# Attention scores on 64-row tiles: a pair of heads in two banks instead of against half-empty keys

## The chip, the core and the metric

The kernel runs on one core of a Trainium2 chip. Times are microseconds of device time. The core has five engines that run side by side and meet through semaphores: TensorE (PE in the rows; its weight loads are PEld), VectorE (DVE), ScalarE (ACT), GpSimd (POOL) and SyncE (SP), which issues DMAs. TensorE writes to PSUM, which has eight banks of 512 floats per partition.

## What is computed

Eight sequences of 256 tokens with 128 channels go through one causal attention layer (16 heads of 8 channels) and then through six layers of local attention and a gated feed-forward. The change lies in the local attention:

```python
# per layer: 16 heads, DIM_HEAD 64, WINDOW 32, n = 256 tokens, QK_SCALE 8
q = l2norm(q) * qs ; k = l2norm(k) * ksc          # then rotary tables on both
bk2, bv2 = look(bk), look(bv)                     # each window sees the one before and itself: 64 keys
mask = (it < jb) | (it > jb + w) | (jb == -1)
sim = jnp.einsum('bhwie,bhwje->bhwij', bq, bk2) * QK_SCALE
sim = jnp.where(mask, -jnp.finfo(sim.dtype).max, sim)
attn = jax.nn.softmax(sim, -1)
out = jnp.einsum('bhwij,bhwje->bhwie', attn, bv2)
```

## The kernel before

A first stage (to about 260 us) computes the causal attention and prepares the weights of the six layers: split in two parts for the projections, the value weights folded with the output weights. Then come 48 units, one for each layer and sequence, `u = (m, s)`. Every engine has a hand-written `step(m, s)` that lists its work for several units at once: while unit `u` makes its scores, `after` is already projected, `before` is in its softmax and values, and `last` is in the feed-forward. The steps of all 48 units are written out one behind the other, and nothing but this order and the semaphores decides when something runs.

In a unit tokens are handled in two tiles `t` of 128. For each: `proj` (L1462 to L1464) makes queries, keys and values in 512-column pieces in the two projection banks; ScalarE squares them (`sq`, L1283), VectorE multiplies by the rotary tables (`rot`, L1136) and sums squares (`ssum`, L1112), GpSimd turns and normalises (L1031, L1050 to L1056, L1072), and `transpose_qk` (L1479) turns each pair of heads over into the bank TP. A pair is 128 rows: 64 channels of one head above 64 of the other. ScalarE copies these out: queries to `qT` (L1305), keys to `kT` (L1311).

The keys are stored twice as wide as they are. `kT` is `[P, 2, PAIRS, WIN + T]`: plane 0 holds the first head's keys in rows 0 to 63 and zeros below, plane 1 the second head's in rows 64 to 127 and zeros above. So one matmul over all 128 rows and 128 columns of keys gives both heads' scores side by side:

```python
out_s = ps[32 * k:32 * k + 32, SO[t] + a // 4, (a % 4) * P:(a % 4 + 1) * P]
last = M.matmul(out_s, qT[:, par, a, 32 * w:32 * w + 32], kT[:, :, a, 32 * w:32 * w + 64], ...)
```

`scores(u, t)` does that for 8 pairs `a` and 4 windows `k`; each window's 32 queries are one 32-column strip of the array. Every float32 matmul is two instructions in the trace (x64 for the 32 of a call). Ahead of them two matmuls in bf16 (L1492), one on rows 0 to 63 and one on rows 64 to 127, write the mask into the two banks `SO[t]` and `SO[t] + 1`, and the scores are added to it. A call waits for the copy of the keys (`qkT_a`) and for the output of the unit before to have left the bank (`o_a`, L1338).

The softmax runs in PSUM and `prob`: VectorE takes the maxima (L1147), subtracts them (L1156), ScalarE takes the exponentials back into the banks (L1319), VectorE sums (L1164, L1166) and scales into `prob` (`soft_scale`, L1173). `transpose_p` (L1507) turns `prob` over pair by pair and `values` (L1518) multiplies with the values. The feed-forward has three products with the first weights (`feed_w1`, L1568), each followed by `gate` on ScalarE (L1377) and `hid` on VectorE (L1214), and `feed_w2` (L1579). The fold of the first stage (L726) multiplies 64-row halves of two weights, the two halves in turn, into two banks.

## Time and profile before

| | us |
|---|---|
| median of 3 runs | 1781.34 (1781.17 to 1782.97) |
| the profiled execution | 1780.26 |
| its span, first to last instruction | 1778.4 |
| TensorE busy | 1708.9 (96%) |
| VectorE busy | 1512.6 (85%) |
| GpSimd busy | 1355.7 (76%) |
| ScalarE busy | 1350.4 (76%) |
| DMA, mean | 149 GB/s |

Busy time is the share in which at least one instruction of the engine is recorded. The ends of matmuls are modelled, so the distance from one start to the next tells more of TensorE than its busy share; the chain of work that ended last gives each instruction the time to the next step, so its rows can be added up. In the rows below, the first number of a timeline or chain row is the start, the second the duration.

### The profile page before, as it was taken

What the parts mean: (1) busy time and instruction counts of PE and PEld (TensorE: products, weight loads), DVE (VectorE), ACT (ScalarE), POOL (GpSimd) and SP (SyncE); (2) the same over time, 40 slices, a digit from 0 to 9 for tenths busy, and PEclk for the clock granted to TensorE, in tenths of its full rate; (3) what the DMA queues carried; (4) which work ended last, traced back from release to release, by engine and by line L of the source; (5) the groups of instructions that cost most, each with busy time, mean ns of one, the idle gap of its engine ahead of it and who ended that gap; (6) DMA issues with size and microseconds to landing.
All of it is one profiled execution on the core that took longest, in us unless ns stands there. A gap on an engine that the chain in (4) does not pass through costs nothing.

```text
span 1778.4 us, 53112 instructions
## 1 busy us (share of the span) xinstructions
PE 1708.9 (96%) x20416; PEld 1355.0 (76%) x20416; DVE 1512.6 (85%) x2297; ACT 1350.4 (76%) x2689; POOL 1355.7 (76%) x2035
## 2 busy tenths in 40 slices
PE   7999968999999999999999999999999999999986
PEld 5666646888888888788888788887888888888864
DVE  5666648999999999999999999999899999999973
ACT  6777846787777777787777788787777887777763
POOL 6767658878788787778878787878878787887850
PEclk9999989999999999999999999999999999999996
DMA  3567706465865646765566656558464666656462
GB/s 115 184 234 262 254 10 159 107 148 120 223 141 132 145 107 139 213 143 139 123 147 191 152 123 146 124 127 236 112 161 104 149 177 168 147 117 146 109 152 63
DMA packets 101340, 264.54 MB, mean 149 GB/s; under 512 B 26720, under 2 KB 34912, under 8 KB 101088
## 3 DMA queue, kind: packets, MB, share of 16 engines
q1 hardware_dynamic: 101088, 261.13, 57.8%
q8 instruction: 164, 2.69, 0.7%
q14 instruction: 88, 0.72, 0.1%
HBM read 45.02 MB, written 27.26 MB: 41 GB/s over the span
## 4 chain that ended last, share of the span: by engine, by line
PE 81%; issue 2%; DVE 1%; ACT 1%; POOL 1%; POOLq 0%; ACTq 0%; DVEq 0%
PE ps L1462 12%; PE ps L1497 10%; PE ps L1479 10%; PE ps L1464 10%; PE ps L1463 10%; PE ps L1518 9%; PE ps L1568 7%; PE ps L1507 5%; PE ps L1579 3%; PE ps L1492 2%; PE ps L1537 1%; PE ps L1545 1%; DVE rot L1136 1%; PE ps L1554 1%; PE ps L1529 1%
## 5 line engine op out<-in xcount | busy, mean ns | idle before, releaser
L1136 DVE TENSOR_TENSOR rot<-ps,rope_l 128x1024 f32<-128x1024 f32 x384 | 461.8, 1213 | 100.9 <-ACT sq L1283 84.8
L1031 POOL TENSOR_TENSOR rot<-rot 128x512 f32<-128x512 f32 x384 | 485.8, 1288 | 31.5 <-DVE rot L1136 31.5
L1293 ACT ACTIVATE un<-ps 128x512 f32<-128x512 f32 x384 | 224.6, 598 | 237.9 <-PE ps L1464 229.8
L1462 PE MATMUL ps<-w_t,xs_hi 128*128 128x512 f32 x768 | 374.9, 488 | 12.5 <-DVE rot L1136 7.6
L1072 POOL TENSOR_TENSOR rot<-rot,rnorm 128x1024 f32<-128x1024 f32 x192 | 365.5, 1904 | 21.3
L1464 PE MATMUL ps<-w_t,xs_lo 128*128 128x512 f32 x768 | 304.7, 397 | 0.0
L1463 PE MATMUL ps<-w_t,xs_hi 128*128 128x512 f32 x768 | 303.6, 395 | 0.0
L1283 ACT ACTIVATE sq<-ps 128x512 f32<-128x512 f32 x384 | 229.1, 597 | 34.6 <-PE ps L1464 20.1
L1311 ACT ACTIVATE kT<-ps 64x512 f32<-64x512 f32 x384 | 226.3, 589 | 23.7 <-PE ps L1479 20.3
L1479 PE MATMUL ps<-ident_s,rot 128*128 128x128 f32 x1536 | 234.8, 275 | 8.6 <-ACT kT L1311 3.4
L1112 DVE TENSOR_REDUCE ssum<-sq 128x16 f32<-128x1024 f32 x192 | 232.5, 1211 | 9.8 <-ACT sq L1283 9.8
L1479 PEld LDWEIGHTS ps<-ident_s,rot 128*128 128x128 f32 x1536 | 182.1, 140 | 65.4 <-issue 28.6
L1462 PEld LDWEIGHTS ps<-w_t,xs_hi 128*128 128x128 f32 x768 | 145.7, 190 | 67.9 <-issue 28.8
L1518 PE MATMUL ps<-vk,pT 128*32 128x128 f32 x6144 | 188.3, 275 | 0.0
L1497 PE MATMUL ps<-kT,qT 128*32 128x128 f32 x6144 | 187.6, 274 | 0.0
L1050 POOL TENSOR_TENSOR newton<-rnorm 128x32 f32<-128x32 f32 x288 | 68.6, 238 | 147.3 <-DVE rnorm L1122 132.3
L1497 PEld LDWEIGHTS ps<-kT,qT 128*32 128x32 f32 x6144 | 161.8, 110 | 21.7 <-issue 21.7
L1518 PEld LDWEIGHTS ps<-vk,pT 128*32 128x32 f32 x6144 | 162.3, 110 | 16.7 <-issue 16.3
L1464 PEld LDWEIGHTS ps<-w_t,xs_lo 128*128 128x128 f32 x768 | 145.1, 189 | 33.8
L1568 PE MATMUL ps<-xg,w_s 128*128 128x256 f32 (+1 forms) x576 | 151.9, 387 | 4.5 <-DVE hid L1214 3.5
L1463 PEld LDWEIGHTS ps<-w_t,xs_hi 128*128 128x128 f32 x768 | 147.2, 192 | 8.0
L1568 PEld LDWEIGHTS ps<-xg,w_s 128*128 128x128 f32 (+1 forms) x576 | 103.3, 180 | 32.6 <-DVE hid L1214 5.9
(121 smaller groups left out, 3093.2 us busy)
## 6 DMA issues: line engine op xcount, KB each, us to landing
vk<-un SPq DMA_DIRECT2D x1440, 128.0 KB, 2.3
w_t<-weights_dram SPq DMA_DIRECT2D x48, 512.0 KB, 6.9
weights_dram<-u_split SPq DMA_DIRECT2D x12, 1024.0 KB, 5.1
weights_dram<-qk_split SPq DMA_DIRECT2D x24, 512.0 KB, 4.0
raw<-wqk_dram SPq DMA_DIRECT2D x24, 256.0 KB, 4.9
wvt_s<-wvt_dram SPq DMA_DIRECT2D x12, 256.0 KB, 4.3
wo_s<-wo_dram SPq DMA_DIRECT2D x12, 256.0 KB, 4.7
w_s<-w_dram SPq DMA_DIRECT2D x6, 341.0 KB, 3.8
```

The costliest lines, as they stand in the source:

```text
L1031: last = G.tensor_tensor(cos[:, :, s, :], cos[:, :, s, :], sin[:, :, 1 - s, :], ALU.add)
L1072: G.tensor_tensor(v, v, rnorm[:, t, kind * H:(kind + 1) * H, None].broadcast_to([P, H, D]), ALU.mult).then_inc(nrm_g.sem, 1)
L1112: V.tensor_reduce(ssum[:, t, kind * H:(kind + 1) * H], sq[:, kind, :].rearrange("p (h e) -> p h e", h=H), AX_X, ALU.add).then_inc(ss_d.sem, 1)
L1136: V.tensor_tensor(dst, src[:, None, :, :].broadcast_to([P, 2, H // 2, D]), tab[:, :, None, :].broadcast_to([P, 2, H // 2, D]), ALU.mult).t ...
L1283: S.activation(sq[:, kind, half * 512:(half + 1) * 512], ps[:, PJ + PJ_BANK[t][2 * kind + half], :], ACT.Square).then_inc(sq_a.sem, 1)
L1462: M.matmul(bank, x_hi, w_t[:, j, 0, :], start=True, stop=False)
L1463: M.matmul(bank, x_hi, w_t[:, j, 1, :], start=False, stop=False)
L1464: last = M.matmul(bank, x_lo, w_t[:, j, 0, :], start=False, stop=True)
L1479: last = M.transpose(ps[:, TP, a * P:(a + 1) * P], rot[:, kind, 0, c * P:(c + 1) * P], ident_s[:, :])
L1497: last = M.matmul(out_s, qT[:, par, a, 32 * w:32 * w + 32], kT[:, :, a, 32 * w:32 * w + 64], start=False, stop=a % 4 == 3)
L1518: last = M.matmul(ps[32 * k:32 * k + 32, SO[t], 0:C], pT[:, a, 32 * k:32 * k + 32], vk[:, 4 * t + k, a, :], start=a == 0, stop=a == PAIRS - 1)
L1568: last = M.matmul(ps[0:rows, FB, g * T:(g + 1) * T], w1_s[:, g * DI + at:g * DI + at + rows], xg[:, :], start=True, stop=True)
```

## The change

The keys lose their empty halves: `kT` is `[P, PAIRS, WIN + T]`, and both heads' keys are copied in one instruction. The mask and the scores are computed per window and per head half, each instruction on 64 rows and 32 columns of the array. A head half has a bank of its own (`SO[t] + hp`), so the banks' order is now head half, pair, key, where it was pair, head half, key. `soft_scale` puts `prob` back into the old order, so that what follows finds it as before. The maxima, sums and reciprocals stay in the banks' order on both sides. Only the part that is zeroed in front of the first window of the keys remains of the two memsets.

```diff
-        kT = sb("kT", [P, 2, PAIRS, WIN + T])
+        kT = sb("kT", [P, PAIRS, WIN + T])
...
-                    G.memset(kT[:, 0, :, :], 0.0)
-                    G.memset(kT[:, 1, :, :], 0.0)
+                    G.memset(kT[:, :, 0:WIN], 0.0)
...
-                    V.tensor_tensor(prob[:, t, :].rearrange("p (h k) -> p h k", h=H), tile_scores(t),
-                                    linv[:, t, :, None].broadcast_to([P, H, 2 * WIN]), ALU.mult).then_inc(pn_d.sem, 1)
+                    pairs = prob[:, t, :].rearrange("p (a hp k) -> p hp a k", hp=2, a=PAIRS)
+                    inv = linv[:, t, :].rearrange("p (hp a) -> p hp a", hp=2)[:, :, :, None].broadcast_to([P, 2, PAIRS, 2 * WIN])
+                    V.tensor_tensor(pairs, tile_scores(t).rearrange("p (hp a) k -> p hp a k", hp=2), inv, ALU.mult).then_inc(pn_d.sem, 1)
...
-                        for hp in range(2):
-                            rows = slice(64 * hp, 64 * hp + 64)
-                            last = S.activation(kT[rows, hp, pairs, WIN + t * P:WIN + (t + 1) * P], src[rows], ACT.Copy)
+                        last = S.activation(kT[:, pairs, WIN + t * P:WIN + (t + 1) * P], src, ACT.Copy)
...
-                    for hp in range(2):
-                        rows = slice(64 * hp, 64 * hp + 64)
-                        M.matmul(ps[:, SO[t] + hp, :], wpick[rows, t, :], wmask[rows, :, :].rearrange("p a k -> p (a k)"), start=True, stop=False)
+                    for k in range(4):
+                        for hp in range(2):
+                            rows = slice(64 * hp, 64 * hp + 64)
+                            M.matmul(ps[32 * k:32 * k + 32, SO[t] + hp, :], wpick[rows, t, 32 * k:32 * k + 32], wmask[rows, :, :].rearrange("p a k -> p (a k)"),
+                                     start=True, stop=False)
                     for a in range(PAIRS):
                         for k in range(4):
                             w = 4 * t + k
-                            out_s = ps[32 * k:32 * k + 32, SO[t] + a // 4, (a % 4) * P:(a % 4 + 1) * P]
-                            last = M.matmul(out_s, qT[:, par, a, 32 * w:32 * w + 32], kT[:, :, a, 32 * w:32 * w + 64],
-                                            start=False, stop=a % 4 == 3)
+                            for hp in range(2):
+                                rows = slice(64 * hp, 64 * hp + 64)
+                                out_s = ps[32 * k:32 * k + 32, SO[t] + hp, a * 2 * WIN:(a + 1) * 2 * WIN]
+                                last = M.matmul(out_s, qT[rows, par, a, 32 * w:32 * w + 32], kT[rows, a, 32 * w:32 * w + 64],
+                                                start=False, stop=a == PAIRS - 1)
```

On TensorE, around the first call of `scores` in a unit: the first hidden-layer product, the masks, the scores and the two projections behind them. Before:

```order
L1568 MATMUL ps<-xg,w_s 128x256 [waits xh_d,w1_in]
L1568 MATMUL ps<-xg,w_s 128x256
L1492 MATMUL ps<-wmask,wpick 128x512 [waits o_a,qkT_a]
L1492 MATMUL ps<-wmask,wpick 128x512
L1497 MATMUL ps<-kT,qT 32x128 x32
L1462 MATMUL ps<-w_t,xs_hi 128x512 [waits rope_d]
L1463 MATMUL ps<-w_t,xs_hi 128x512
L1464 MATMUL ps<-w_t,xs_lo 128x512
```

After, at the same place (the lines below L1310 have moved by two, L1492 is L1491, L1497 is L1499, L1568 is L1570):

```order
L1570 MATMUL ps<-xg,w_s 128x256 [waits xh_d,w1_in]
L1570 MATMUL ps<-xg,w_s 128x256
L1491 MATMUL ps<-wmask,wpick 32x512 [waits o_a,qkT_a]
L1491 MATMUL ps<-wmask,wpick 32x512 x7
L1499 MATMUL ps<-kT,qT 32x64 x64
L1460 MATMUL ps<-w_t,xs_hi 128x512 [waits rope_d]
L1461 MATMUL ps<-w_t,xs_hi 128x512
L1462 MATMUL ps<-w_t,xs_lo 128x512
```

Nothing moved; two masks became eight and 32 matmuls of 128 columns became 64 of 64.

On ScalarE, between the exponentials of the first token tile and the copy of the values: the last bank of keys, which the second call of `scores` waits for, and the output `o`. Before:

```order
L1319 ACTIVATE ps<-prob 128x1024 [waits sub_d]
L1311 ACTIVATE kT<-ps 64x4x128 [waits sc_p,qkT_p]
L1311 ACTIVATE kT<-ps 64x4x128
L1338 ACTIVATE o<-ps 128x128 [waits av_p]
L1293 ACTIVATE un<-ps 128x512 [waits vk_in1,u_p0] x2
```

After:

```order
L1317 ACTIVATE ps<-prob 128x1024 [waits sub_d]
L1309 ACTIVATE kT<-ps 128x4x128 [waits sc_p,qkT_p]
L1336 ACTIVATE o<-ps 128x128 [waits av_p]
L1293 ACTIVATE un<-ps 128x512 [waits vk_in1,u_p0] x2
```

One copy stands where two did, and `o` follows it directly.

## Rows read from the trace of the kernel before

**Rows 1.** Per-core view: span and mean granted TensorE clock.

```profile
core 0: 1778.4 us, clock 0.986
```

**Rows 2.** Table of stretches: length, busy of PE, PEld, DVE, ACT, POOL; clock.

```profile
260.00:1748.00 1488.00, 1463.74 (x18347) 1187.58 (x18346) 1344.55 (x1748) 1160.50 (x1989) 1180.18 (x1799) 1.00 0.61 146
...
560.22:591.10 30.88, 30.70 (x388) 25.00 (x386) 28.36 (x38) 24.48 (x42) 24.87 (x39) 1.00 0.60 139
```

**Rows 3.** The page's chain that ended last, by engine and by line.

```profile
PE 81%; issue 2%; DVE 1%; ACT 1%; POOL 1%; POOLq 0%; ACTq 0%; DVEq 0%
PE ps L1462 12%; PE ps L1497 10%; PE ps L1479 10%; PE ps L1464 10%; PE ps L1463 10%; PE ps L1518 9%; PE ps L1568 7%; PE ps L1507 5%; PE ps L1579 3%; PE ps L1492 2%; PE ps L1537 1%; PE ps L1545 1%; DVE rot L1136 1%; PE ps L1554 1%; PE ps L1529 1%
```

**Rows 4.** That chain in order of time, around both calls of one unit.

```profile
908.05 0.32 PE ps L1492 x2
908.37 1.89 PE ps L1497 x64
910.26 0.43 PE ps L1462
...
924.26 0.23 PE ps L1464
924.61 0.39 PE ps L1492 x2
```

**Rows 5.** Timeline of TensorE: masks of two units, and one call's scores.

```profile
907.98 0.39 PE L1492 MATMUL ps<-wmask,wpick 64*128 64x512 bf16 x2
...
924.94 1.95 PE L1497 MATMUL ps<-kT,qT 128*32 128x128 f32 x64
...
938.87 0.39 PE L1492 MATMUL ps<-wmask,wpick 64*128 64x512 bf16 x2
```

**Rows 6.** Waits from 500 to 1500 us: in total, times, longest.

```profile
POOL newton L1050 <- DVE rnorm L1122: 89.3, 65, 1.9
DVE rot L1136 <- ACT sq L1283: 51.4, 32, 2.9
PEld ps L1492 <- ACT kT L1311: 27.9, 65, 0.5
...
DVE ssum L1112 <- ACT sq L1283: 6.9, 33, 0.2
```

**Rows 7.** Timeline, windows ending at 908.35 (PE, PEld) and 908.50 us (PE).

```profile
908.30 0.32 PE L1497 MATMUL ps<-kT,qT 128*32 128x128 f32 x4
...
908.30 0.15 PEld L1497 LDWEIGHTS ps<-kT,qT 128*32 128x32 f32 x7 [0.23 <-issue]
...
908.30 0.43 PE L1497 MATMUL ps<-kT,qT 128*32 128x128 f32 x8
```

**Rows 8.** A fold in the timeline, and all folds by form (busy, mean ns).

```profile
60.18 1.16 PE L726 MATMUL ps<-wo_s,wvt_s 64*128 64x128 f32 x16
...
L726 PE MATMUL ps<-wo_s,wvt_s 64*128 64x128 f32 x192 | 13.9, 285 | 0.0
```

**Rows 9.** Copies of keys and queries (mean; min/median/max ns), one `o`.

```profile
L1311 ACT ACTIVATE kT<-ps 64x512 f32<-64x512 f32 x384 | 226.3, 589 | 23.7 <-PE ps L1479 20.3
...
L1305 ACT ACTIVATE qT<-ps x192: 587/592/613, 252.5 to 1719.7; 128x512 f32<-128x512 f32 x192
...
924.19 0.28 ACT L1338 ACTIVATE o<-ps 128x128 f32<-128x128 f32 x1
```

**Rows 10.** Timeline of GpSimd in the opening stage, behind the memsets.

```profile
35.28 0.19 POOL L378 TENSOR_TENSOR var<-mv,eps 128x2 f32<-128x2 f32 x1 [5.99 <-DVE mv L473]
```

**Rows 11.** Timeline of VectorE and TensorE behind the first call's scores.

```profile
909.39 1.21 DVE L1173 TENSOR_TENSOR prob<-ps,linv 128x1024 f32<-128x1024 f32 x1
910.52 0.47 DVE L1214 SCALAR_TENSOR_TENSOR hid<-ps,cur,gate 128x256 f32<-128x256 f32 x1
...
911.70 1.02 PE L1568 MATMUL ps<-xg,w_s 128*128 128x256 f32 x4
...
914.93 1.23 DVE L1136 TENSOR_TENSOR rot<-ps,rope_l 128x1024 f32<-128x1024 f32 x1 [1.54 <-ACT sq L1283]
```

## The prediction

> **What bounds the kernel now.** I read the per-core view first: one core, span 1778.4 us [rows 1]. That execution took 1780.26 us in all, 1.9 us more than its span and 1.1 us under the median of the three timed runs, 1781.34. The table of stretches comes next [rows 2]: the 48 units of the six layers lie between 260 and 1748 us, at the full granted clock (1.00), and TensorE is busy 1463.74 of 1488 us there. VectorE has 1344.55, ScalarE 1160.50, GpSimd 1180.18. The stage before (260 us) and the end (30 us) hold no score work but the first and last calls, so the change is decided in those 1488 us. TensorE's busy time is modelled, so I check it against the chain of work that ended last: 81% of the span is TensorE [rows 3], and in a unit its pieces follow each other with hardly a hole [rows 4]. The scores stand in that chain with 10% (L1497) and 2% (L1492). One unit takes 30.89 us: the masks of two units start at 907.98 and 938.87 [rows 5].
>
> TensorE is not far ahead of VectorE. In one period VectorE is busy 28.36 of 30.88 us [rows 2]. Over 1000 us (32.4 units) it waits 51.4 us in its rope line for ScalarE's squares and 6.9 us in its sums [rows 6]: 1.80 us per unit. If every such wait vanished, a unit would still take 30.89 - 1.80 = 29.1 us. That is the floor any TensorE saving meets.
>
> **What a call costs now.** A unit has two calls of `scores`. In the chain, the mask step has 0.32 us, the 64 matmul instructions of L1497 (32 calls in float32, each two instructions) have 1.89 us, and then the next projection starts [rows 4]: 2.21 us. The 64 run as rounds of four. Four start inside 0.05 us, eight need 0.11 us more [rows 7], so 16 rounds of 0.109 us make 1.75 of the 1.89, and 0.14 us is getting in and out. A round is one instruction on each of the four 32-column tiles, 128 moving columns each, half of them made only to meet zeros.
>
> **Part 1, the scores on eight tiles.** Each matmul now has 64 rows and 64 moving columns; there are 128 instructions per call on eight tiles (two row halves by four column strips), so 16 per tile as before. Half the columns give 0.055 us per round; eight starts at the 7 ns that separate starts within a round (seven weight loads begin inside 0.05 us [rows 7]) give 0.056. 16 x 0.056 = 0.90 us in place of 1.75. Does the array run two row halves at once? The trace has the case: in the fold (L726) 16 float32 instructions on two 64-row tiles, into two banks, in the same order as here (both passes of one half, then both of the other), take 1.16 us from first start to last end [rows 8]. Take away the last one's 0.27 to 0.285 and some 0.88 us is left. One after the other they would need 15 x 0.109 = 1.64 us; in pairs, 7 x 0.109 plus the first weight load = 0.87. So they ran in pairs. The masks say the same: two of 512 columns on the two row halves, and the scores start 0.32 us behind them, where one projection of 512 columns takes 0.23 in the chain and two in sequence would take 0.46 [rows 4].
>
> What no row shows is eight tiles in flight with a steady supply. The lower bound is the 7 ns per load-and-matmul pair of rows 7. The upper bound is the fastest pace shown over a whole call: 1.95 us for 64 pairs with a tail of 0.27, some 27 ns per pair [rows 5], and there the array was the limit, not the supply. I take 7 to 10 ns, since the four starts within a round and the fold's are the nearest rows; the 27 ns end is a rival below.
>
> The Trainium skill, "TensorE: Matmul & The Clock Gate" (section "Wait — 56ns, not 53.3ns?"), says that start-to-start never drops below about 25 ns however small the matmul. By that rule as an estimate a call of 128 would take 128 x 25 = 3.2 us, and the change would lose. Rows 7 show starts 7 ns apart on different tiles, against the rule as a general one.
>
> **Part 2, the masks.** Eight instructions of 512 columns on the same eight tiles replace two with 128 columns of weights. Run together they take the 0.23 us of one 512-column step and 7 x 0.007 = 0.05 us: 0.28. They no longer differ in tile shape from the scores, so the turn between the shapes, part of the 0.32 now, goes. A call becomes 0.28 + 0.90 + 0.14 = 1.32 us: 0.89 saved, 1.8 per unit. If masks of the same column strip ran in sequence they would cost 0.46, and a call saves 0.7.
>
> **Part 3, keys.** ScalarE writes a bank of keys in one 128 x 512 copy where it had two of 64 rows (L1311): each of these takes 0.59 us, and so does the 128-row copy of the queries (L1305) [rows 9]. Four copies per unit go: 2.4 us of ScalarE, off the path as time, but the last bank of keys is there 0.59 us earlier. TensorE waits for it: 27.9 us in 65 calls, longest 0.5 [rows 6]. Most of that waiting of the weight loads is covered by the matmuls before. In the chain the second mask of a unit has 0.39 instead of 0.32 and begins 0.35 after its forerunner instead of 0.23 [rows 4]: 0.19 us per unit that goes. There `o` (L1338, 924.19 + 0.28) ends last [rows 9], and it is queued on ScalarE behind the keys, so it moves up with them.
>
> **Part 4, the small ones.** VectorE's scaling (L1173) writes with a stride per head half: same elements, rows of 64 floats, taken at its present 1.21 us [rows 11]; a tenth more would be 0.24 us per unit. Two memsets in the opening stage shrink to a small one; GpSimd waits 5.99 us for VectorE soon after them, so that gains nothing [rows 10]. No queue's order changes.
>
> **The sum.** TensorE: 1.8 + 0.19 = 2.0 us per unit, to 28.9. But VectorE's floor is 29.1, GpSimd's at most 28.1 (89.3 us of waits for VectorE in 32.4 units, 2.8 each [rows 6], can go), ScalarE's far lower. So VectorE becomes late next. Before 914.93 it waits 1.54 us for the square of the next unit's first projection [rows 11]; that wait is what the shorter call uses up. With two engines within 0.2 us of their floors and each waiting for the other over two projection banks, I do not expect either floor to be met: I take 1.45 of the 1.80, a unit of 29.45. Times 46 units (the first and last are filled by latencies, not by TensorE) = 66.7 us. 1780.3 - 66.7 = 1713.6, and 1.1 to the median: **1715 us**. Its own range: 1.1 to 1.8 per unit, 1698 to 1731.
>
> **Rivals.**
> (a) The two order-bound engines fit badly: with scores shorter, TensorE reaches the second hidden-layer product while VectorE still has the scaling and `hid` (910.52 + 0.47) before it [rows 11]; product 2 started at 911.70, so 0.7 us of room is there and a saving of 0.9 is more than it. If such places leave only half the gain, 0.5 to 1.1 per unit: 1731 to 1758. Chance 0.17.
> (b) The eight tiles do not overlap by halves: two rounds of four of 0.055 each, 32 rounds, 1.76 us, nothing gained, with only 0.19 us per unit from the keys, 9 us: 1772, or 1760 to 1777. The fold speaks against it, but it had two tiles, not eight. Chance 0.07.
> (c) Slower: supply of instructions. Twice as many pairs must be fetched and issued, and if a pair costs 27 ns whatever its tile, 136 pairs take 3.7 us in place of 2.2: 1.5 x 94 = 141 us, minus the 9 of the keys: 1912. It decides from 2.2 / 136 = 16 ns per pair upward; at 20 ns a call is 2.7 us and the time 1780 + 47 - 9 = 1818. For it: no row shows a call supplied faster. Against: starts of 7 ns. Chance 0.10.
> (d) The wait is only exchanged: VectorE's waits are of a kind that stays (its own longer strided write, later squares) and the time stays within 0.2%. Chance 0.03.
> That leaves 0.63 for the forecast.
>
> **Numbers.** 0.2% (3.6 us) is about what a measurement of this kernel can tell. Faster: 0.63 + 0.17 + 0.07 = 0.87, less 0.01 for (b) at its upper end: 0.86. Same: 0.04. Slower: 0.10. The range takes in the forecast and (a): 1697 to 1758.
>
> **What would show it.** Right: L1499 with 128 instructions in 1.1 to 1.3 us from first start to last end (1.95 now), the masks' line before them 0.28 in the chain, a period near 29.45, VectorE's wait for squares down from 51.4 us to under 15 and new TensorE waits for VectorE (rope, `hid`). TensorE's granted clock stays 1.00. Rival (a): the same short call, but a period over 29.8 and more idle TensorE. Rival (b): rounds of four, 1.9 us. Rival (c): a call over 2.2 us with even gaps between starts, VectorE waiting more. The forecast is wrong if VectorE shows busy time per unit over 28.6, or waits that no shorter call removes.

## The result: 1769.7 us, and the profile after

The changed kernel takes 1769.7 us, the median of six runs (1763.5 to 1774.7); the kernel before, in six runs beside it, 1781.3 (1778.9 to 1783.0). The ratio is 0.9936, 95% interval 0.9914 to 0.9958: faster by 0.4 to 0.9%, where 3.7% were predicted. The profiled execution took 1769.3 us.

The per-core view and the page of the changed kernel. Scores are now L1499, masks L1491, projections L1460 to L1462. First the span and clock; then, from the page, busy time with its share, then the chain that ended last by engine and by line, then the groups of the scores (busy, mean ns | idle before, releaser), last the DMA queue that brings instructions (packets, MB, share):

```profile
core 0: 1767.4 us, clock 0.984
```

```profile
PE 1671.2 (95%) x27136; PEld 1330.4 (75%) x27136; DVE 1506.8 (85%) x2297; ACT 1234.8 (70%) x2497; POOL 1354.1 (77%) x2034
...
PE 79%; issue 4%; DVE 2%; POOL 1%; ACT 1%; POOLq 0%; ACTq 0%; DVEq 0%
...
L1499 PE MATMUL ps<-kT,qT 64*32 64x64 f32 x12288 | 152.6, 225 | 27.5 <-issue 27.5
...
L1499 PEld LDWEIGHTS ps<-kT,qT 64*32 64x32 f32 x12288 | 146.9, 105 | 35.6 <-issue 29.6
...
q8 instruction: 216, 3.54, 0.9%
```

Against [rows 3], "issue" has gone from 2% to 4% of the chain. "Issue" is time in which the engine waited for nothing that the profile shows. Added up over the chain it went from 44.0 to 68.1 us, and 27.5 us of it now stand before score matmuls, where there was none. That was not in the prediction.

The table of stretches, the layers and one undisturbed unit (columns as in [rows 2]):

```profile
260.00:1748.00 1488.00, 1433.35 (x25087) 1166.76 (x25085) 1342.99 (x1759) 1046.25 (x1800) 1183.31 (x1803) 0.99 0.61 146
903.89:933.66 29.77, 29.75 (x526) 24.36 (x526) 28.03 (x38) 22.18 (x39) 24.82 (x38) 1.00 0.59 135
```

An undisturbed unit takes 29.77 us where it took 30.88 [rows 2], and TensorE is busy all of it. So the change did save 1.12 us per unit, and over 46 units that would be 51 us. But only 28 of the 46 units are undisturbed. I call a unit so if no two successive matmul starts in it lie over 0.9 us apart; 43 of 46 were before. Gaps of over 0.7 us between two matmul starts, from 262 to 1700 us, sum to 48.7 us in 31 places, where the kernel before had 10.1 us in 8. So 39 of the 51 us went there; 51 - 39 leaves 12, and the spans differ by 11.0. The clock takes a small share as well: behind three of the longest gaps (2.4 us to 723.9, 4.4 us to 970.5, 2.4 us to 1539.4) the granted TensorE clock is 0.50 for 3.4 us, the lower of its two levels (1.2 GHz), where the kernel before has none below 1.00 between 252 and 1737 us. These three units are 1 to 2 us longer than their gaps explain. A fourth gap of 2.4 us, to 1462.8, has no such stretch behind it. The table of stretches behind the 4.4 us:

```profile
970.50:973.90 3.40, 3.35 (x20) 2.61 (x21) 2.45 (x2) 0.60 (x1) 3.32 (x3) 0.50 0.03 12
```

The timeline of TensorE, for one call that runs through and one that does not:

```profile
903.89 0.41 PE L1491 MATMUL ps<-wmask,wpick 64*32 64x512 bf16 x8
904.12 1.46 PE L1499 MATMUL ps<-kT,qT 64*32 64x64 f32 x128
905.50 0.51 PE L1460 MATMUL ps<-w_t,xs_hi 128*128 128x512 f32 x1
...
964.83 0.41 PE L1491 MATMUL ps<-wmask,wpick 64*32 64x512 bf16 x8
965.06 1.34 PE L1499 MATMUL ps<-kT,qT 64*32 64x64 f32 x115
970.55 0.46 PE L1499 MATMUL ps<-kT,qT 64*32 64x64 f32 x13 [4.15 <-issue]
```

The second call stops after 115 of its 128 score matmuls, stands for 4.15 us, the longest such stall of this kernel, and then does the last 13. Twenty of the 96 calls contain such a stop, of 0.7 us upward; from start to start they sum to 31.8 us. The waits show the same (in total, times, longest; 260 to 1748 us):

```profile
PEld ps L1499 <- issue: 29.6, 19, 4.3
PE ps L1499 <- issue: 27.5, 20, 4.1
```

The kernel before has no such stop in any call.

The call that runs through is slower than predicted, too. The same timeline cut off at successive times says how many score matmuls had started by 904.15, 904.20, 904.26, 904.31, 904.45, 904.89 and 905.33 us:

```profile
904.12 0.24 PE L1499 MATMUL ps<-kT,qT 64*32 64x64 f32 x8
904.12 0.29 PE L1499 MATMUL ps<-kT,qT 64*32 64x64 f32 x16
904.12 0.34 PE L1499 MATMUL ps<-kT,qT 64*32 64x64 f32 x20
904.12 0.40 PE L1499 MATMUL ps<-kT,qT 64*32 64x64 f32 x25
904.12 0.56 PE L1499 MATMUL ps<-kT,qT 64*32 64x64 f32 x36
...
904.12 1.01 PE L1499 MATMUL ps<-kT,qT 64*32 64x64 f32 x81
904.12 1.42 PE L1499 MATMUL ps<-kT,qT 64*32 64x64 f32 x126
```

The first 16 start as foretold, eight at once every 0.055 us. From there to 905.33 us 110 start in 1.13 us, one per 10.3 ns. Eight tiles took eight pairs per 0.055 us at the start of the call; now they get five in that time.

### The profile page after: what moved, and what is told of

It is laid out like the page before. It is cut to its first block, busy times and chain, and to the rows that moved or that the text cites. A ratio compares the mean times of both kernels' runs of the same rounds, so it can differ in the third digit from the quotient of the medians.

```text
span 1767.4 us, 66359 instructions
## 1 busy us (share of the span) xinstructions
PE 1671.2 (95%) x27136; PEld 1330.4 (75%) x27136; DVE 1506.8 (85%) x2297; ACT 1234.8 (70%) x2497; POOL 1354.1 (77%) x2034
## 3 DMA queue, kind: packets, MB, share of 16 engines
q8 instruction: 216, 3.54, 0.9%
## 4 chain that ended last, share of the span: by engine, by line
PE 79%; issue 4%; DVE 2%; POOL 1%; ACT 1%; POOLq 0%; ACTq 0%; DVEq 0%
PE ps L1460 12%; PE ps L1477 10%; PE ps L1462 10%; PE ps L1461 10%; PE ps L1520 10%; PE ps L1499 7%; PE ps L1570 7%; PE ps L1509 5%; PE ps L1581 3%; PE ps L1491 2%; PE ps L1539 1%; PE ps L1547 1%; DVE rot L1135 1%; PE ps L1556 1%; PE ps L1531 1%
## 5 line engine op out<-in xcount | busy, mean ns | idle before, releaser
L1293 ACT ACTIVATE un<-ps 128x512 f32<-128x512 f32 x384 | 229.8, 598 | 316.0 <-PE ps L1462 260.0
L1460 PE MATMUL ps<-w_t,xs_hi 128*128 128x512 f32 x768 | 376.6, 490 | 18.2 <-DVE rot L1135 8.6
L1462 PE MATMUL ps<-w_t,xs_lo 128*128 128x512 f32 x768 | 307.0, 400 | 0.0
L1477 PE MATMUL ps<-ident_s,rot 128*128 128x128 f32 x1536 | 238.4, 278 | 5.7 <-POOL rot L1071 3.1
L1460 PEld LDWEIGHTS ps<-w_t,xs_hi 128*128 128x128 f32 x768 | 146.6, 191 | 64.5 <-DVE rot L1135 18.9
L1499 PE MATMUL ps<-kT,qT 64*32 64x64 f32 x12288 | 152.6, 225 | 27.5 <-issue 27.5
L1499 PEld LDWEIGHTS ps<-kT,qT 64*32 64x32 f32 x12288 | 146.9, 105 | 35.6 <-issue 29.6
L1462 PEld LDWEIGHTS ps<-w_t,xs_lo 128*128 128x128 f32 x768 | 146.0, 190 | 36.1 <-issue 1.8
L1570 PE MATMUL ps<-xg,w_s 128*128 128x256 f32 (+1 forms) x576 | 153.1, 389 | 5.1 <-DVE hid L1214 4.0
L1146 DVE TENSOR_REDUCE smax<-ps 128x16 f32<-128x1024 f32 x96 | 116.9, 1217 | 17.2 <-PE ps L1499 17.1
L1570 PEld LDWEIGHTS ps<-xg,w_s 128*128 128x128 f32 (+1 forms) x576 | 99.8, 180 | 38.2 <-DVE hid L1214 11.9
```

The costliest lines, as they stand in the source:

```text
L1293: S.activation(un[:, (u[1] % 2) * TT + t, j // 2, (j % 2) * HALF:(j % 2 + 1) * HALF], ps[:, PJ + PJ_BANK[t][QK_BANKS + j], :], ACT.Copy).t ...
L1460: M.matmul(bank, x_hi, w_t[:, j, 0, :], start=True, stop=False)
L1462: last = M.matmul(bank, x_lo, w_t[:, j, 0, :], start=False, stop=True)
L1477: last = M.transpose(ps[:, TP, a * P:(a + 1) * P], rot[:, kind, 0, c * P:(c + 1) * P], ident_s[:, :])
L1499: last = M.matmul(out_s, qT[rows, par, a, 32 * w:32 * w + 32], kT[rows, a, 32 * w:32 * w + 64], start=False, stop=a == PAIRS - 1)
L1570: last = M.matmul(ps[0:rows, FB, g * T:(g + 1) * T], w1_s[:, g * DI + at:g * DI + at + rows], xg[:, :], start=True, stop=True)
```

## Where a call lies in the stream of instructions

The stalls are not spread evenly. I counted the instructions of TensorE's compiled program up to each call (a load and a matmul are one each, and a call of masks and scores has 272). The page's queue of instructions has 216 packets for 3.54 MB, 16.4 KB each. The trace has 27136 weight loads, 27136 matmuls and 1119 other instructions of TensorE, which makes 256 per packet; in the kernel before it is 41951 for 164 packets, 256 again. Counted in blocks of 256, a call that began at position 190 to 240 of its block stalled, 18 of 18 times; of the 78 others two did. Every stall ended at the same place of the stream, position 206 or 207. A unit has 1064 instructions, 40 more than four blocks, so its calls drift through the block and a group of them is hit every six units or so.

**Theory.** TensorE's instructions come in blocks of 256, each needing a microsecond or more (most packets of q8 in the trace took 0.9 to 1.5 us). Elsewhere 256 instructions last many microseconds. A call uses 272 in 1.5 us. If it begins late in a block it runs through the rest, through the next block, and dry. **Rivals:** it waits for data or a bank that the profile does not name; the copies' DMA traffic delays it; or the stalls were there before and only moved.

The times of the q8 packets in the changed kernel's trace speak for the theory. In each of the 20 stalled calls the first matmul behind the stop starts 1.2 to 1.6 us after a q8 packet has ended. Counted in order, that packet is always the one that brings the block at whose beginning TensorE stopped, and it had begun only after TensorE entered the block before: 1.1 us later in the median of all blocks, in some 4 us later and more. So TensorE does not stop only if it spends longer on a block than that delay, the packet's own 0.9 to 1.5 us and some 1.3 us more. At the stops it had used up its block in 1.4 to 4.5 us; the exception is the very first call of the layers, where the packet began 11.4 us after TensorE entered the block before.

### The same work, moved in the stream

The phase of a call can be changed without touching it. A projection is three matmuls of 512 columns; written as six of 256 it does the same work and has six more instructions. The table says how many projections are halved ahead of which call:

```diff
+SPLIT = {7: 9, 17: 8, 27: 9, 37: 8, 47: 9, 57: 9, 67: 8, 77: 9, 87: 9}
...
+                    pieces = 1
+                    if SPLIT.get(calls[0], 0) > done.get(calls[0], 0):
+                        done[calls[0]] = done.get(calls[0], 0) + 1
+                        pieces = 2
+                    for piece in range(pieces):
+                        c = slice(piece * (HALF // pieces), (piece + 1) * (HALF // pieces))
+                        M.matmul(bank[:, c], x_hi, w_t[:, j, 0, c], start=True, stop=False)
...
```

Three tables: no call in the window (78 projections halved), 46 calls in it (476 halved), and the latter with 11 more halved in the opening, which shifts all later calls by 66 and leaves 7 in it.

> The changed kernel, but 78 of its 768 projections are made in two halves of 256 columns, three more load-and-matmul pairs each, placed ahead of nine calls of scores. Nothing else changes. In the changed kernel's trace 20 of 96 calls hold a stall of 0.7 to 4.4 us (31.8 us in all), and every one of these calls begins with its first instruction at a place from 191 to 238 in TensorE's instruction stream counted modulo 256; calls that begin elsewhere hold none. Theory (supply): TensorE gets its instructions in blocks of 256, and a call of 272 instructions that runs through a whole block faster than the next one arrives stops for it. The 78 halved projections move all 96 calls out of that range, so the stalls go: 1767 less 32, some 1733 to 1745 us, calls 1.24 to 1.40 us from first to last start. Rival (data): the stalls come from DMA traffic or from a neighbour engine at certain times of a layer, and moving instructions leaves them: 20 or so stalls, 1765 to 1775 us. Rival (price): the extra halves cost more than they save: stalls gone, over 1760 us.

> The changed kernel with 476 of its projections made in two halves of 256 columns, placed so that 46 of the 96 calls begin from 190 to 240 modulo 256 in TensorE's instruction stream. Theory (supply): some 46 stalls of 1.2 to 2 us in the calls, 60 to 90 us in all, so 1795 to 1830 us, slower than the kernel before. Rival (data): some 20 stalls, and a time near 1770 plus whatever 476 halved projections cost, the same as in the run with 487 of them that is sent along.

> The kernel of the run before with 11 more halved projections in the opening of the loop, 487 in all, and none moved. By count 7 calls then begin from 190 to 240 modulo 256 instead of 46. Theory (supply): some 7 stalls, 45 to 75 us faster than its twin, near 1740 to 1755 us. Rival (data): the same time as its twin, within 5 us.

Measured: 1742.2 us, ratio 0.979 (0.9775 to 0.9804); 1812.0 us, 1.0182 (1.0159 to 1.0206); 1760.6 us, 0.9912 (0.9883 to 0.9942). The waits of the scores' line (here L1511) from 260 to 1748 us, of the three in this order, with a stalled call of the second behind its own (timeline):

```profile
PEld ps L1511 <- issue: 8.3, 7, 2.2
PE ps L1511 <- issue: 7.2, 5, 2.1
```

```profile
PEld ps L1511 <- issue: 69.7, 45, 4.9
PE ps L1511 <- issue: 62.7, 45, 4.7
```

```profile
920.51 0.41 PE L1503 MATMUL ps<-wmask,wpick 64*32 64x512 bf16 x8
920.74 1.36 PE L1511 MATMUL ps<-kT,qT 64*32 64x64 f32 x117
922.86 0.33 PE L1511 MATMUL ps<-kT,qT 64*32 64x64 f32 x11 [0.77 <-issue]
```

```profile
PEld ps L1511 <- issue: 14.7, 9, 2.3
PE ps L1511 <- issue: 13.2, 9, 2.1
```

Gap by gap, all 46 calls of the second kernel that stood in the window stalled, and none of its other 50. The third is the clean comparison: it has the same halved projections and 11 more, and runs 51 us faster, with 9 stalled calls (15.2 us), six of them among the 7 in the window. All 46 stops of the second kernel end 1.2 to 1.6 us after their q8 packet, as in the changed kernel. In the first, five calls still stall (8.2 us), four at positions 247 to 251 and one at 4, so the window has no sharp end at 240. (The trace of the first is that of its slowest execution, 1756.2 us; the median is 1742.2.) The cause is the position of a dense call in its block, and the first table recovers 28 of the 55 us that the prediction was off.

The control puts the first table into the kernel before:

> The kernel BEFORE the change with one edit, which is the padding of e1_phase_off: 78 of its projections (three matmuls of 512 columns each) are written as six matmuls of 256 columns. Full result. It is the control for e1: if halving projections has a price or a gain of its own, it shows here, where a score call has 64 score matmuls and no stall inside it. Theory (stalls belong to the calls of 272 instructions, the padding only moves them): same as before within 0.2%, 1776 to 1786 us, at most 78 x 6 instructions x 5.5 ns = 2.6 us of cost; call length unchanged at 1.68 us from first to last start. Rival (e1's gain comes from the halves themselves, for instance a shorter tail of a projection): faster by up to the 27 us that e1 won over the changed kernel, near 1755.

Measured 1781.4 us, ratio 0.9995 (0.9983 to 1.0007), with the call as it was:

```profile
884.36 1.95 PE L1509 MATMUL ps<-kT,qT 128*32 128x128 f32 x64
```

Halving projections is worth nothing in itself. A second table with a wider window:

> The changed kernel with another table of halved projections: 102 in place of the 78 of e1_phase_off, at other units, so that no score call begins at position 184 to 255 of a block of 256 instructions in TensorE's stream (e1 left out 190 to 245 and kept calls at 247 to 251, of which three still stalled). Full result. Theory (the stall depends only on where a call begins in its block, and the window reaches from about 190 up to the block's end): at most 2 stalled calls instead of 5, some 5 to 6 us less of stalls than in e1, 24 more halved projections cost at most 0.8 us: 1736 to 1742 us, ratio to before 0.976 to 0.979. Rival (the calls left in e1 stalled because of what shared the queue at that time, not by position): 1742 us or more, ratio 0.979 to 0.983, with stalls at other positions.

Measured 1741.2 us, ratio 0.9769 (0.9751 to 0.9787), the fastest version here. Four calls stall, 6.0 us in all, against five and 8.2 us in the first table. I expected at most two, and the intervals of the two tables overlap. The four begin at positions 16 to 58, far from the window, but their q8 packets are late: three begin 3.2 to 3.8 us after TensorE entered the block before (1.0 us in the median of all blocks), and these three, at 712, 953 and 1435 us, fall into the 10 to 11 us in which the weights of the next layer are being fetched. The fourth is the first call of all. So position alone does not decide; how late the packet begins does too. The waits of the scores' line, and one undisturbed unit in the table of stretches:

```profile
PEld ps L1511 <- issue: 5.7, 4, 1.9
PE ps L1511 <- issue: 5.1, 4, 1.8
```

```profile
877.71:907.43 29.72, 29.72 (x526) 24.39 (x526) 28.13 (x38) 22.01 (x38) 25.05 (x39) 1.00 0.58 132
```

### What holds a call that does not stall

Two experiments on the pace inside a call. The first halves the moving columns, so that each matmul takes less of the array:

```diff
-                                out_s = ps[32 * k:32 * k + 32, SO[t] + hp, a * 2 * WIN:(a + 1) * 2 * WIN]
+                                out_s = ps[32 * k:32 * k + 32, SO[t] + hp, a * 2 * WIN:a * 2 * WIN + WIN]
...
-... kT[rows, a, 32 * w:32 * w + 64],
+... kT[rows, a, 32 * w:32 * w + 32],
```

> The changed kernel with each of the score matmuls on 32 moving columns instead of 64: the second half of each window's keys is left out, so the output is another one. Same instructions, half the streaming. Theory (supply of instructions, one per 5.5 ns): a call's first to last start stays 1.2 to 1.25 us, or 1.35 in the first call of a unit, because after the first 32 pairs the starts already come one pair per 11 ns and not in rounds of eight per 56 ns. Rival (array): the streaming sets the pace, and a call shrinks towards 16 rounds of 0.03 to 0.04 us, 0.7 us. Stalls in some 20 calls stay by the theory, since the instructions stand where they stood; the time is within 8 us of the changed kernel's.

A call on the first tile, in the timeline:

```profile
901.13 1.28 PE L1499 MATMUL ps<-kT,qT 64*32 64x32 f32 x128
```

Measured 1763.9 us, in one run, with some 20 stalls as before. Half the columns take the call from 1.24 us (first to last start) to 1.09: less than the theory had (1.2 to 1.25), and far from the rival's 0.7. Behind the first 24 pairs two start every 16.7 ns, one per 8.4 ns. So the columns account for 0.15 us of the call, and the array is not what holds the rest. That the rest is the rate at which instructions come is the likely reading; no run changed the number of weight loads alone. For it speaks that pairs can start faster when they stand ready: with two masks in place of eight (below) the first 32 pairs start some 7 ns apart, and here the first 24 behind the eight masks start within 0.10 us.

The second keeps the work and changes the order, a tile's 16 matmuls in a row:

```diff
-                    for a in range(PAIRS):
-                        for k in range(4):
-                            w = 4 * t + k
-                            for hp in range(2):
-                                rows = slice(64 * hp, 64 * hp + 64)
+                    for k in range(4):
+                        w = 4 * t + k
+                        for hp in range(2):
+                            rows = slice(64 * hp, 64 * hp + 64)
+                            for a in range(PAIRS):
```

> The changed kernel with one edit: within a call the loops run strip and row half outside and pairs inside, so each of the eight tiles gets its 16 instructions (8 pairs in float32) in a row before the next tile is named, and not one pair on each tile in turn. Same 128 instructions, same work, full result. The question is whether what holds a call now (one load-and-matmul pair per 11 ns after the first 32 pairs) is the supply alone, or the supply together with how far ahead TensorE looks for work on a free tile. Theory A (supply at some 11 ns per pair, look-ahead of a few tens of instructions): the look-ahead reaches two or three tiles, not eight; a tile needs 55 ns per pair, so three tiles in flight give one per 18 ns and the call takes 128 x 18 ns = 2.3 us from first to last start instead of 1.24 to 1.35; 96 calls times 1 us, less what was stalled anyway, puts the time at 1850 us or more. Theory B (look-ahead of a whole call or more, supply decides alone): the call stays at 1.25 to 1.4 us and the time near 1770. Theory C (no look-ahead across tiles): 128 x 55 ns = 7 us per call, time over 2200 us.

A call in the timeline:

```profile
896.65 0.41 PE L1491 MATMUL ps<-wmask,wpick 64*32 64x512 bf16 x8
896.88 5.95 PE L1499 MATMUL ps<-kT,qT 64*32 64x64 f32 x128
```

Measured 2139.9 us, in one run; a call takes 5.74 us from first to last start, 45 ns per pair (one, at the lower clock, 10.2 us). Theory A's look-ahead of two or three tiles (2.3 us) was wrong, and theory C (7 us) is nearer but not right either. The starts repeat every 0.70 us, once per tile of 16 pairs: eight lie 56 ns apart, then eight come within 0.20 us, in two series of 56 ns pushed into one another (670, 726, 781, 837 and 676, 756, 811, 867 ns in the call at 1068.6 us). The rows do not name the tile; I read this as the last four pairs of one tile together with the first four of the next. Then TensorE does look ahead, but only by about four pairs, and it is the turning through the tiles that keeps all eight at work. Also, no call of this kernel stalls: 272 instructions in 6 us are slow enough for the blocks. The stall depends on pace as well as on position.

The next one tests both together. The call is cut in half, and the projection that followed it stands between the halves:

```diff
+                    scores(u, 0, 0)
                     proj(u, 0, 7)
+                    scores(u, 0, 1)
...
+                    scores(u, 1, 0)
                     proj(after, 1, 5)
+                    scores(u, 1, 1)
```

> The changed kernel with each score call written in two halves (pairs 0 to 3 with the masks, then pairs 4 to 7), the projection that followed the call standing between them. Same instructions, no padding, full result. Theory A (two things held the call: after the first 32 load-and-matmul pairs, which are queued ahead, pairs come only every 11 ns; and 272 instructions go through one block of 256 of the stream in less time than the next block needs): each half of 64 pairs starts with a full queue, takes 32 x 7 + 32 x 11 = 0.57 us from first to last start, 1.15 for both in place of 1.24 to 1.39, and with 0.7 us of projection between them the stalls inside calls, 31.8 us in the changed kernel, fall to under 10. Each extra change of tile shape costs about 0.1 us, 0.2 per unit, 9 us in all. Time 1769.7 - 22 - 5 + 9 = 1752 us, 1742 to 1760. Rival B (the stall depends on the position alone, however long the instructions around it take): stalls stay near 32 us, time 1770 to 1780. Rival C (the row maxima come 0.7 us later and VectorE falls behind): undisturbed period over 30.3 us in place of 29.75, with VectorE waiting for the scores' line; time over 1775 even if the stalls go.

The timeline of TensorE around a call on the first tile, then waits from 260 to 1748 us, of the first projection and of the scores' line:

```profile
881.12 0.84 PE L1500 MATMUL ps<-kT,qT 64*32 64x64 f32 x64
882.57 0.50 PE L1460 MATMUL ps<-w_t,xs_hi 128*128 128x512 f32 x1 [0.60 <-DVE rot L1135]
883.46 0.86 PE L1500 MATMUL ps<-kT,qT 64*32 64x64 f32 x64
```

```profile
PE ps L1460 <- DVE rot L1135: 31.9, 49, 1.7
PE ps L1500 <- issue: 7.5, 12, 2.0
```

Measured 1793.6 us, ratio 1.0073 (1.0059 to 1.0087): slower than before, against my 1752. The mechanism came as expected. TensorE's waits before scores fall from 27.5 us to 7.5, which goes against rival B, and behind the projection the second half starts with 32 matmuls at the full 7 ns before it falls to the slower pace. But a first half takes 0.63 us, not 0.57, so nothing is won there. And the undisturbed unit rose from 29.77 to 30.99 us. Rival C had the size and one of its signs (VectorE's waits for the scores go from 17.1 us in 13 places to 49.2 us in 95), but not the main cause. The projection, moved 0.7 us forward, finds its bank not yet read. It waits for VectorE's rotary product (31.9 us in all, 4.2 us in the changed kernel), and once in each unit it starts 0.82 us after the last score, where it follows by 0.15 us otherwise: 0.67 us lost, 31 us over 46 units. The other 0.5 us of the unit's 1.2 I can only place. From the last start of a first half to the first of the second it is 1.04 us even where nothing is waited for, and the projection's three steps of some 0.23 us are 0.7 of them, so going out of the scores' tile shape and back costs some 0.35 us per call, where I had put 0.1. A step moved by less than a microsecond cost nearly as much as all stalls did.

### The smaller parts

The masks on two tiles again, two matmuls with 128 columns of weights for the eight:

```diff
-                    for k in range(4):
-                        for hp in range(2):
-                            rows = slice(64 * hp, 64 * hp + 64)
-                            M.matmul(ps[32 * k:32 * k + 32, SO[t] + hp, :], wpick[rows, t, 32 * k:32 * k + 32], ...)
+                    for hp in range(2):
+                        rows = slice(64 * hp, 64 * hp + 64)
+                        M.matmul(ps[:, SO[t] + hp, :], wpick[rows, t, :], ...)
```

> The changed kernel with part 2 undone: the masks are again two matmuls of 64 rows with 128 columns of weights each, the scores stay on the eight tiles. Full result. A call has 260 instructions in place of 272. Theory A (the turn between tile shapes is what the eight-tile masks saved): 0.32 us from the first mask to the first score start in place of 0.227, 0.19 us more per unit, 9 us in all, minus 0.07 us per call for 12 instructions less in the queue ahead (the first pairs of the scores are then better supplied), so an undisturbed period of 29.75 to 29.95 us. Rival B (no turn: the scores of a tile start when the mask of its rows is through): 0.23 us as now, the period 0.07 to 0.14 lower, 29.6 to 29.7. The stalls fall at other places since every call has 12 instructions less (a unit 24 less, so its position in a block drifts by +16 in place of +40): their sum is not comparable, between 10 and 60 us, and the time 1745 to 1800 us; the period and the mask-to-score time are what this run is for.

A call in the timeline, masks and scores:

```profile
902.84 0.39 PE L1490 MATMUL ps<-wmask,wpick 64*128 64x512 bf16 x2
903.16 1.49 PE L1497 MATMUL ps<-kT,qT 64*32 64x64 f32 x128
```

From mask to score 0.320 us in place of 0.227 in every call, as theory A had it: the turn costs 0.093 us more than the eight masks do. The undisturbed unit takes 29.88 us, 0.11 more. The time is 1768.2 us, with 17 stalled calls (one stop of them 0.5 us) and 22.8 us at other positions, so it says nothing of the masks.

The keys copied in two pieces again, on top of the first table, so that the stalls are few:

```diff
-                        last = S.activation(kT[:, pairs, WIN + t * P:WIN + (t + 1) * P], src, ACT.Copy)
+                        for hp in range(2):
+                            rows = slice(64 * hp, 64 * hp + 64)
+                            last = S.activation(kT[rows, pairs, WIN + t * P:WIN + (t + 1) * P], src[rows], ACT.Copy)
```

> e1_phase_off with part 3 of the change undone: ScalarE writes each bank of keys in two copies of 64 rows in place of one of 128 rows. Same addresses, same TensorE stream (so the same few stalls), full result. The prediction put 0.19 us per unit of TensorE's waiting on it, 9 us in all. Theory A (it was worth that): 1742 + 9 = 1751 us, ratio to before 0.984. Theory B (the keys are never late once other things wait longer): 1742 within 3 us, ratio 0.979. Theory C (ScalarE is now behind more often, since VectorE waits 44 us for its squares in 1000 us and each of 4 extra copies of 0.59 us per unit delays them): the whole 2.4 us of a unit cannot be hidden, and the time rises by 0.5 us per unit or more, 1765 us and over.

The masks' wait for the keys, 260 to 1748 us, and a unit in the table of stretches:

```profile
PEld ps L1505 <- ACT kT L1314: 39.9, 88, 1.8
```

```profile
880.60:910.66 30.06, 29.86 (x525) 24.57 (x526) 28.31 (x38) 24.52 (x43) 25.01 (x39) 1.00 0.57 130
```

Measured 1758.1 us, ratio 0.9864 (0.9839 to 0.9889) against 0.979 with one copy: 13 us. The undisturbed unit takes 30.02 us where it takes 29.80 with one copy, 0.22 us, so 10 of the 13 us are those of theory A, and the wait of the masks for the keys is back.

### The second call of a unit, which stayed open

The call on the first tile of a unit takes 1.242 us from first to last start, to 0.002 us the same each time; that on the second tile takes 1.32 to 1.60, median 1.39. The former has no data packet beside it except around a change of layer, each of the latter has some 100. So I shrank the copies of the values, once in their bytes and once in their packets too:

```diff
-                                src = un[32 * k:32 * k + 32, (n % 2) * TT + tile, hp, :]
-                                sp.dma_start(vk[lo:lo + 32, w, :, :].rearrange("p a c -> p (a c)"),
-                                             src).then_inc(vk_in[t].sem, 16)
+                                src = un[32 * k:32 * k + 32, (n % 2) * TT + tile, hp, 0:C]
+                                sp.dma_start(vk[lo:lo + 32, w, 0, :], src).then_inc(vk_in[t].sem, 16)
```

The second of the two kernels has one row in place of the 32:

```diff
+                                src = un[32 * k:32 * k + 1, (n % 2) * TT + tile, hp, 0:C]
+                                sp.dma_start(vk[lo:lo + 1, w, 0, :], src).then_inc(vk_in[t].sem, 16)
```

> The changed kernel with a part of its data movement left out: each of the 30 copies per unit that put the values next to each other (un to vk, 128 KB each) moves only its first pair's 128 of 1024 columns, 16 KB, so the result is not the reference's. TensorE's stream is the same, instruction for instruction, and so are all waits and the number of copies. In the changed kernel the call at the first tile of a unit takes exactly 1.242 us from first to last start and has no data packet beside it; the call at the second tile takes 1.32 to 1.60 us and has about 100 packets beside it. Theory A (these copies slow the supply of instructions): the second call falls to 1.242 to 1.27 us, about 0.15 us per unit, 7 us in all. For the stalls A splits in two: A1 (a block of instructions needs its 1.0 to 1.3 us even on a quiet queue, and a call that begins 190 to 240 instructions into a block runs dry in any case): still about 18 to 20 stalled calls, 0.7 to 1.3 us each, 18 to 25 us in all, time 1752 to 1762 us. A2 (the fetch is late because of the copies' packets): under 8 stalled calls, under 10 us, time 1740 to 1748. Rival B (the second call is slower for another reason, such as engines that read the same memory): it stays at 1.39 and the time at 1764 to 1770 us.

> As e12_small_copies, which left out seven eighths of every row that the value copies move and kept their 32 rows (so the packets were as many, but small); here each copy moves 128 columns of one row only, so both bytes and packets are nearly gone. The result is not the reference's. TensorE's stream, the waits and the number of copies are the same. e12 left the second call of a unit at 1.397 us with about 99 packets beside it. Theory A (the number of packets beside a call slows it, not their bytes): the second call falls to 1.24 to 1.27 us, like the first one, which has no packet beside it. Rival B (the second call is slower for a reason that has nothing to do with the copies): it stays at 1.39 us. The stalls are not expected to change from e12's 19 calls and 26 us: each needs the 1.0 to 1.3 us of a block of instructions in any case. Time 1745 to 1756 us.

The waits of the scores' line in the first of the two, then the timeline of one second and one first call, of each kernel:

```profile
PEld ps L1498 <- issue: 23.9, 18, 3.4
PE ps L1498 <- issue: 22.2, 19, 3.2
```

```profile
912.78 1.57 PE L1498 MATMUL ps<-kT,qT 64*32 64x64 f32 x128
926.62 1.46 PE L1498 MATMUL ps<-kT,qT 64*32 64x64 f32 x128
```

```profile
910.22 1.53 PE L1498 MATMUL ps<-kT,qT 64*32 64x64 f32 x128
924.05 1.46 PE L1498 MATMUL ps<-kT,qT 64*32 64x64 f32 x128
```

Measured 1755.9 and 1756.4 us, in two runs each. The second call stayed at 1.40 and 1.45 us (median from first to last start; the rows add the last one's own time). So neither the bytes of these copies nor most of their packets slow it; 34 to 97 other packets still lie beside it in the last kernel, and those I did not take away. The cause of this 0.15 us per unit is open. For the stalls the two say more: 19 and 20 calls still stall, 26.3 and 26.6 us in all. A block needs its time with most of these bytes gone as well, and the copies lengthen the stalls by only 5 us in sum, A1 rather than A2 (A1 had 18 to 25 us). The stalls do not account for all of the 14 us between these kernels and the changed one: gaps of over 0.7 us, inside calls and outside, fall from 48.7 us to 39.4 and 37.0, and the other 2 to 5 us have no name.

## Why the prediction was right or wrong

**What bounds** held, and more firmly than I used it. TensorE is busy 29.75 of the 29.77 us of an undisturbed unit.

**Part 1, the scores, is a step that failed**, in the term 16 x 0.056 = 0.90 us, which is 7 ns per load-and-matmul pair. That pace holds for the 16 pairs that start right behind the masks; after that a pair comes every 10.3 ns. The call's starts span 1.24 us on the first tile and 1.39 on the second, not 0.90. The prediction named "7 to 10 ns", and 128 x 10 ns = 1.28 us would have been the call; the sum went by the lower end alone. I had taken the price from four starts within one round [rows 7] and from a fold of 16 instructions [rows 8]: both are bursts no longer than the 32 pairs that started at full pace in the runs above, and neither shows a sustained pace. The row halves do run at the same time, as [rows 8] said; rival (b) is out. The rule of the Trainium skill ("TensorE: Matmul & The Clock Gate", section "Wait — 56ns, not 53.3ns?") that start-to-start never drops below about 25 ns is not borne out across tiles either: 10.3 ns sustained, 3 to 4 ns between starts of one round.

**Part 2** was right in kind and gave a little more than forecast: 0.28 us predicted for the masks where 0.32 was, 0.227 measured from mask to score, 0.19 per unit by the starts and 0.11 by the period where the masks were put back. **Part 3** was right: 0.19 us per unit forecast, 0.22 measured by the unit's period. The copy is one instruction of 0.595 us. None of [rows 6]' 27.9 us of waiting is put down to the keys any more, but the masks' loads still stand idle 22.6 us from 500 to 1500 us, now on "issue", so that sum was no measure of the gain. **Part 4** was right:

```profile
L1309 ACT ACTIVATE kT<-ps x192: 579/595/609, 259.0 to 1716.3; 128x512 f32<-128x512 f32 x192
...
L1174 DVE TENSOR_TENSOR prob<-ps,linv x96: 1209/1224/1226, 277.5 to 1729.1; 128x1024 f32<-128x1024 f32 x96
```

The strided write takes what the dense one took [rows 11].

**The sum** of a unit, with the measured terms: scores 1.682 - 1.242 = 0.44 and 1.682 - 1.39 = 0.29, masks 0.19, keys 0.22, together 1.14; measured 1.12. Predicted were 2.0, cut to 1.45 by VectorE's floor. The floor of 29.1 us was never reached. The cut did some good by accident, since it hid part of the error in the scores: they gave 0.73 us per unit where 1.7 were predicted, 1.0 missing, and only 0.33 per unit, 15 us, shows in the time. That is luck. In the list of what would show it, VectorE's wait for squares was to fall from 51.4 us [rows 6] to under 15, and it is 44.4:

```profile
DVE rot L1135 <- ACT sq L1283: 44.4, 32, 3.5
```

That line was the plainest sign that VectorE still has room and TensorE still bounds.

**The stalls**, 39 us more in gaps, are the larger miss: the sum has no term for them, so it put the supply of instructions at nothing. 31.8 of the 39 us are stops inside the calls. Rival (c) named the mechanism, the supply of instructions, but as a price of each pair ("decides from 16 ns per pair"). It came in other forms: likely as a pace of 10.3 ns, too fast for its point of decision (8.4 with half the columns; that this is supply was argued, not shown), and surely as a break at blocks of 256 instructions, which no row of the kernel before shows in a call of 132 instructions, since there it never ran dry. What could have been seen: the kernel before brings its instructions in 164 packets, and the change adds 64 pairs of scores and 6 of masks to each of 96 calls. The page of the kernel before (packets, MB, share):

```profile
q8 instruction: 164, 2.69, 0.7%
```

I priced the added instructions one at a time and never asked for how many in a row.

**The number.** 1715 predicted, 1769.7 measured, 55 us off: 15 from the scores' pace and about 39 from stalls. Without the 39 us of gaps the time would be 1731, at the lower edge of rival (a)'s range, 1731 to 1758, and for another reason than its own. That the time would fall was right.

## What to carry to other kernels

Splitting matmuls over more tiles trades array time for instructions, and the second has a sustained price that a short burst does not show: here 10.3 ns per load and matmul, and a stall of 0.7 to 4.4 us where some 270 instructions pass in 1.5 us across the end of a block. Where a profile shows "issue" before a dense burst, count where the burst stands in the engine's stream, and try a few harmless extra instructions ahead of it: here they were worth 28 us of 1770. And a price is taken from a row as long as the thing it prices.

## What was not expected of the hardware

- Instructions of TensorE arrive in blocks of 256 (q8: 216 packets, 3.54 MB, most of them 0.9 to 1.5 us each), the packet of a block begins only after TensorE has entered the block before (1.1 us after, in the median), and work goes on 1.2 to 1.6 us after the packet's end where TensorE stood waiting for it. A burst of 272 in 1.5 us runs dry if it begins at position 190 to 240 of a block: 46 of 46 calls where it was provoked. Copies with an eighth of the bytes leave it so (19 calls, 26.3 us).
- The longest stall of the changed kernel, 4.15 us, comes where a layer changes and seven weight transfers of 512 KB are under way; the four longest of the kernel with 46 calls in the window, 3.6 to 4.9 us from start to start, do so too. Such gaps are found outside the calls as well (in the fastest version at 472 us, 3.4 us). The block's own packet then takes no longer, 0.94 us, but it begins 4.6 us after TensorE entered the block before, in place of 1.1. That it is held up by the weights was not tested.
- Pairs on different tiles overlap only if they stand near each other in the program, within about four pairs by the spacing of the starts: in turn 10.3 ns per pair, tile by tile 45 ns.
- A turn between tile shapes, two masks of 64 rows by 128 columns and then scores of 64 by 32, takes 0.093 us more than eight masks in the scores' own shape.
